# Wider token tiles and a swapped copy of the queries in the first stage of a vision tower

## The chip, the cores and the metric

The kernel runs on one core of one Trainium2 chip. The metric is device time in microseconds for one execution of the whole program; three runs of the kernel before gave 3623.95 to 3631.38 us, median 3631.38.

## The reference

Sixty-four images of 224 x 224 become 196 tokens each (patches of 16 x 16 x 3, 768 values, embedded to 256 channels), then comes one attention block with a relative-position term and one mixture-of-experts block. What the first stage has to compute is this, cut to what matters:

```python
h = einsum('bnp,dp->bnd', patches, W) + b                     # h0
x = layernorm(h)
Q, K, V = x @ Wq, x @ Wk, x @ Wv                              # 16 heads of 16 dims
term1 = einsum('bhqd,bhkd->bhqk', Q, K)
term2 = einsum('bhqd,kd->bhqk', Q, r)                         # r: sin and cos of the distance
term3 = einsum('hd,bhkd->bhk', u, K)
term4 = einsum('hd,kd->hk', v, r)
scores = (term1 + term3 + rel_shift(term2 + term4)) / sqrt(16)
```

Since r holds sines and cosines of a distance, the terms on r are computed as a rotation of the query: each dimension of Q + v is multiplied by one table, its partner dimension (8 further on, modulo 16) by another, and the two products are added. Everything is handed on as a bf16 high half and a bf16 low half, so that three bf16 products give nearly fp32.

## The kernel before

`tower` runs six stages one after the other; `project` (L112) is the first and the only one that the diff touches. It works through 32 positions of 392 tokens (two images, PAIR). Each engine has its own list of instructions, written by hand, with waits on semaphores; nothing reorders them. `positions` (L194) runs `position(n, u)` for n = 0 to 32, u = n modulo 2 choosing the buffer. In a position the engines do the following, in the order of their lists.

- TensorE: transposes the normalised rows xn(n) into psT (L457); embeds the tokens of n + 1 (four tiles of 98 tokens, 72 products of 256 columns, into psH); sums per head the products of Q + u with the next token's key for n - 1 (L469, into a corner of psT called psC); then values V(n) into psJ1 (24 products of 256 columns), keys K(n) into psJ0 (12 of 392), and per half m of the channels the queries and the queries with swapped dimensions (L472 onward, 24 of 392). The swapped queries come from a second set of weight columns.
- ScalarE: casts psT to nh, splits the next x into its high half xh, casts the rotated halves of n - 1 (L288), copies V to v32 (L294), casts K (L300), takes the standard deviation for n + 1 (L273), copies K in fp32 (k32), casts the queries (QH, L309).
- VectorE: nl = psT - nh; xl = x - xh (L334); then `normalise(n + 1)`: adds the token bias to psH, giving h0 (L339), statistics, their aggregation (L343, L349), waits for ScalarE's standard deviation, takes the reciprocal and writes xn with four `tensor_scalar` instructions (L356); copies psC to c32 (L371); then `rotate(n)`: per half m four terms from the two query tiles in PSUM (L385), the products with the shifted keys (L393) and the low half of the query (L397).
- GpSimd: low half of K (L416), and per half m the sum of the terms (L419) and, after ScalarE's cast, its low half (L421).
- The SP queue: stores of h0 and of v, the load of x for n + 4, the store of c, and last the store of the stack of rotated halves, each as soon as its wait allows, in this order (L227 to L240). So the store of h0 for n waits in the queue behind the stack of n - 1.

Two of VectorE's waits decide the order around the change: h0 of n + 1 may only be written when the store of n - 1 has landed, and rotate of n only starts when GpSimd has written the low halves of n - 1:

```python
dve.wait_ge(h0_out.sems[u], h0_out.at(n - 2, u))
dve.wait_ge(abl_ok.sem, abl_ok.at(n - 1))
```

At the start ScalarE waits for all seven weight and table loads before its first cast.

## Time and profile before

| what | value |
|---|---|
| median of three runs | 3631.38 us (3623.95 to 3631.38) |
| profiled execution | 3636.08 us, span 3634.4 us |
| mean granted TensorE clock | 0.939 |
| busy over the span: TensorE, VectorE, ScalarE, GpSimd | 89%, 72%, 41%, 45% |
| first stage | from 0 to about 675 us |

The page divides the span into 40 slices; the first seven, some 640 us, are the first stage, with TensorE at nine tenths or more from the second on. A share over the whole span says little about this stage, so windows and the timeline of the stage itself are read. A busy time on the timeline is from the start of an instruction to its end, and instructions of one engine that follow each other may overlap by some 0.1 us; where a sum matters, the spacing of starts is used.

### The profile page before, as it was taken

The page shows a single profiled execution, that of the slowest core. Times are in us where ns is not written, and L with a number is a line of the kernel's source. Part 1 is how long each engine was busy: PE and PEld are TensorE (multiplying, and loading weights), DVE is VectorE, ACT ScalarE, POOL GpSimd, SP SyncE. Part 2 cuts the span into 40 slices and gives each one's busy share as a digit, 9 for nine tenths or more (in the row PEclk, how much of TensorE's full clock was granted, in tenths as well). Part 3 has the DMA queues.
Part 4 walks back from the last instruction along what each step waited for, and adds up shares of the span by engine and source line. Part 5 has one row for each costly group of instructions (what it writes and reads, how often), then busy time and mean ns, then how long its engine had stood idle before and what let it go on. Part 6 is the DMA issues. An engine that isn't in the chain of part 4 may idle for free. (4 is left out here: it accounts for less than half of the span.)

```text
span 3634.4 us, 89293 instructions
## 1 busy us (share of the span) xinstructions
PE 3229.9 (89%) x34825; PEld 2526.0 (70%) x34881; DVE 2623.7 (72%) x6129; ACT 1498.6 (41%) x2991; POOL 1617.8 (45%) x1965
## 2 busy tenths in 40 slices
PE   6999999399999999999996722999599999998997
PEld 6888887378888888888883311778377777775876
DVE  5888888568888888888884676554266666665887
ACT  3444444056666666666663310332133333332221
POOL 2555555256666666666662010577200000004776
PEclk9999999579999999999998855999799999998999
DMA  4666665736556565665654611354333333225776
GB/s 141 185 185 197 195 186 161 189 84 164 157 149 172 136 166 148 160 162 148 170 133 131 182 30 34 110 140 126 95 116 111 107 104 106 95 90 135 217 219 165
DMA packets 449244, 518.11 MB, mean 143 GB/s; under 512 B 64150, under 2 KB 418804, under 8 KB 448397
## 3 DMA queue, kind: packets, MB, share of 16 engines
q1 hardware_dynamic: 427376, 473.19, 46.1%
q0 software_dynamic: 21504, 39.94, 4.1%
...
q14 instruction: 119, 0.97, 0.1%
HBM read 306.93 MB, written 215.94 MB: 144 GB/s over the span
## 5 line engine op out<-in xcount | busy, mean ns | idle before, releaser
L1281 POOL DMA_INDIRECT sb_ye<-scratch_ye,sb_table x224 | 240.8, 1075 | 805.6 <-DMA sb_gw<-scratch_gw 733.3
L854 DVE TENSOR_REDUCE p_mx<-p_psS 98x2 f32<-98x390 f32 (+1 forms) x1024 | 527.1, 556 | 0.0
L800 ACT ACTIVATE p_after<-p_psF 98x392 f32<-98x392 f32 x512 | 255.1, 498 | 480.6 <-PE p_psF L946 472.5
L803 ACT ACTIVATE p_probs<-p_psE 98x392 f32<-98x392 f32 x1024 | 450.1, 496 | 0.0
L848 DVE COPY_PREDICATED p_psS<-p_later,p_psD 98x196 f32<-98x196 uint32 x1024 | 330.6, 362 | 120.0 <-PE p_psS L932 111.4
L749 POOL TENSOR_SCALAR_AFFINE_SELECT p_after<-p_after 98x392 f32<-98x392 f32 x512 | 274.4, 536 | 243.2 <-ACT p_after L800 243.0
L1269 POOL DMA_INDIRECT scratch_xe<-sa_xs,sa_table x224 | 222.2, 992 | 205.6 <-DMA sa_xs<-scratch_xf 140.4
L753 POOL TENSOR_SCALAR_AFFINE_SELECT p_probs<-p_probs 98x392 f32<-98x392 f32 x512 | 274.5, 536 | 85.8 <-ACT p_probs L803 80.2
L969 PE MATMUL p_psO<-p_probs,p_v 98*32 98x196 f32 x4096 | 279.8, 345 | 2.0 <-POOL p_probs L753 1.7
L419 POOL TENSOR_TENSOR p_rt<-p_rt 128x784 f32<-128x784 f32 x64 | 187.1, 2924 | 122.7 <-DVE p_st L397 122.7
L103 PE MATMUL p_psH<-p_wh,p_xh 128*98 128x256 bf16 x768 | 211.5, 275 | 24.3 <-DVE p_xl L334 24.3
L916 PE MATMUL p_psD<-p_K,p_U 96*98 96x98 bf16 (+1 forms) x2048 | 187.8, 215 | 36.7 <-DVE p_later L835 29.0
L916 PEld LDWEIGHTS p_psD<-p_K,p_U 96*98 96x98 bf16 x2048 | 160.6, 128 | 73.4 <-DVE p_later L835 29.1
L103 PE MATMUL p_psH<-p_wl,p_xh 128*98 128x256 bf16 x768 | 211.3, 275 | 0.0
L103 PE MATMUL p_psH<-p_wh,p_xl 128*98 128x256 bf16 x768 | 211.2, 275 | 0.0
L946 PE MATMUL p_psF<-p_U,p_K 98*98 98x98 bf16 x2048 | 180.3, 211 | 28.8 <-DMA p_U<-p_mrow 28.8
L1387 DVE CAST ex_gh<-ex_g 128x512 bf16<-128x512 f32 (+1 forms) x256 | 106.3, 415 | 106.7 <-ACT ex_g L1322 87.4
...
L1389 DVE TENSOR_TENSOR ex_gl<-ex_g,ex_gh 128x512 bf16<-128x512 f32 (+1 forms) x256 | 171.4, 669 | 8.8
L1322 ACT ACTIVATE ex_g<-ex_psG,ex_b 128x512 f32<-128x512 f32 (+1 forms) x128 | 85.7, 669 | 219.7 <-PE ex_psG L103 219.7
L1322 ACT ACTIVATE ex_g<-ex_psG,ex_first_b 128x512 f32<-128x512 f32 (+1 forms) x128 | 85.7, 669 | 218.1 <-PE ex_psG L103 218.1
L946 PEld LDWEIGHTS p_psF<-p_U,p_K 98*98 98x98 bf16 x2048 | 147.5, 127 | 32.5 <-DMA p_U<-p_mrow 31.6
(300 smaller groups left out, 10110.7 us busy)
## 6 DMA issues: line engine op xcount, KB each, us to landing
...
```

The lines of the kernel that those rows point to most:

```text
L103: last = nc.tensor.matmul(out, a, b, start=start and k == 0, stop=stop and k == len(todo) - 1)
L749: nc.gpsimd.affine_select(after[c][:], after[c][:], pattern=[[0, 4], [-1, TILE]], compare_op=ALU.is_ge, fill=nothing, base=-2, channel_mul ...
L753: nc.gpsimd.affine_select(diagonal, diagonal, pattern=[[0, 4], [1, TILE]], compare_op=ALU.is_ge, fill=nothing, base=0, channel_multiplier= ...
L800: act.activation(after[c][:].rearrange("p h t -> p (h t)"), psF[:, 0:4 * TILE], ACT.Exp, scale=DK ** -0.5).then_inc(p_ok.sem, 1)
L803: act.activation(probs[c][:, b, :], psE[:, b, 0:PAIR], ACT.Exp, scale=DK ** -0.5).then_inc(p_ok.sem, 1)
L848: nc.vector.copy_predicated(own[:, :, c * TILE:(c + 1) * TILE], later[:].unsqueeze(1).broadcast_to([TILE, 2, TILE]), upper).then_inc(chose ...
L854: nc.vector.tensor_reduce(mx[g1][:, c, 4 * q1 + 2 * b:4 * q1 + 2 * b + 2], own, AX.X, ALU.max).then_inc(s_max.sem, 1)
L916: last = nc.tensor.matmul(psD[:, j * TILE:j * TILE + wide], U[u][0:STACK, h][:, mid], K[u][0:STACK, h][:, mid.start + 1:mid.start + 1 + wi ...
L946: last = nc.tensor.matmul(psF[:, j * TILE:(j + 1) * TILE], K[u][0:ROWS, h][:, mid], U[u][0:ROWS, h][:, mid], start=True, stop=True)
L969: nc.tensor.matmul(psO[32 * j:32 * j + 32, 0:S], v32[u][:, 2 * g + c, 4 * q + j, :], probs[c][:, j // 2, (j % 2) * S:(j % 2 + 1) * S], sta ...
L1269: nc.gpsimd.indirect_dma_start(out=d["xe"], out_offset=bass.IndirectOffsetOnAxis(ap=table[:, b * BLOCK + t, k:k + 1], axis=0), in_=xs[v][: ...
L1281: nc.gpsimd.indirect_dma_start(out=ye[v][u][:, t, k, :], out_offset=None, in_=d["ye"], in_offset=bass.IndirectOffsetOnAxis(ap=table[:, at ...
```

## The change

The embedding, the statistics and the values now work on tiles of 112 tokens: even positions bring in four tiles (448 tokens), odd ones three (336). nh and nl become one ring of two positions: `new[u]` is what a position brings in, `own[u]` the 392 tokens whose keys and queries it computes. TensorE no longer computes the swapped queries; the weight columns for them stay in memory unused. Since the dimensions lie eight heads apart, the partner dimension lies 64 partitions away, and ScalarE makes the swapped copy `qsw` in SBUF with two activations of 64 partitions per half m. The keys are cast from k32, after the queries.

The rows' normalisation goes from VectorE to ScalarE: VectorE makes the reciprocal and the shift nmr = -mean x rstd, ScalarE writes xn with scale and bias. VectorE's rotation of n - 1 now lies in position n, its first half ahead of nl(n), its second behind it, and the moments come before xl. GpSimd adds both halves' terms before it subtracts either. At the start the token weights and the first x are loaded ahead of the rest, and the first embedding waits for their casts alone.

VectorE, one position in the loop (p_h is h0, p_psJ the queries, p_rt the terms, p_st the stack). Before:

```order
L363 TENSOR_TENSOR p_nl<-p_psT,p_nh 128x784
L334 TENSOR_TENSOR p_xl<-p_x,p_xh 128x2352
L339 TENSOR_TENSOR p_h<-p_psH,p_tokb 98x1024
L343 BN_STATS p_stats<-p_h 98x6 x4
L349 BN_AGGR p_mv<-p_stats 98x2 x4
L352 RECIPROCAL p_rstd<-p_std 98x4
L356 TENSOR_SCALAR p_xn<-p_h,p_mv,p_rstd 98x256 x4
L371 COPY p_c<-p_psT 98x64
L385 SCALAR_TENSOR_TENSOR p_rt<-p_psJ,p_cols,p_rot 128x392 x4
L393 SCALAR_TENSOR_TENSOR p_prod<-p_psJ,p_cols,p_k 128x392
L397 SCALAR_TENSOR_TENSOR p_st<-p_psJ,p_cols,p_st 128x392
```

And now, from nl on:

```order
L386 TENSOR_TENSOR p_nl<-p_psT,p_nh 128x2x336
L401 REGISTER_ALU
L407 SCALAR_TENSOR_TENSOR p_prod<-p_psJ,p_cols,p_k 128x392
L404 SCALAR_TENSOR_TENSOR p_rt<-p_psJ,p_cols,p_rot 128x392 x2
L415 MEMSET p_prod 128x4
L416 SCALAR_TENSOR_TENSOR p_st<-p_psJ,p_cols,p_st 128x392
L404 SCALAR_TENSOR_TENSOR p_rt<-p_qsw,p_cols,p_rot 128x392 x2
L357 ISA
L359 TENSOR_TENSOR p_h<-p_psH,p_tokb 112x1024
L363 BN_STATS p_stats<-p_h 112x6 x4
L368 BN_AGGR p_mv<-p_stats 112x2 x4
L373 RECIPROCAL p_rstd<-p_std 112x4
```

The second half of the rotation stands between nl and the bias addition, the four xn instructions are gone, and two of the terms read p_qsw.

ScalarE, one position in the loop. Before:

```order
L281 ACTIVATE p_nh<-p_psT 128x784
L268 ACTIVATE p_xh<-p_x 128x2352
L288 ACTIVATE p_st<-p_rt 128x2x392
L294 ACTIVATE p_v<-p_psJ 98x1024
L288 ACTIVATE p_st<-p_rt 128x2x392
L300 ACTIVATE p_st<-p_psJ 128x2x392
L273 ACTIVATE p_std<-p_mv,p_eps 98x4
L306 ACTIVATE p_k<-p_psJ 128x2x392
L309 ACTIVATE p_st<-p_psJ,p_cols 128x392 x2
```

And now, from the standard deviation of one position to nh of the next:

```order
L282 ACTIVATE p_std<-p_mv,p_eps 112x3
L309 ACTIVATE p_v<-p_psJ 112x1024
L288 ACTIVATE p_xn<-p_h,p_nmr,p_rstd 112x256 x3
L317 ACTIVATE p_k<-p_psJ 128x2x392
L321 ACTIVATE p_st<-p_psJ,p_cols 128x392
L324 ACTIVATE p_qsw<-p_psJ 64x392
L325 ACTIVATE p_qsw<-p_psJ 64x392
L321 ACTIVATE p_st<-p_psJ,p_cols 128x392
L324 ACTIVATE p_qsw<-p_psJ 64x392
L325 ACTIVATE p_qsw<-p_psJ 64x392
L327 ACTIVATE p_st<-p_k 128x2x392
L297 ACTIVATE p_nh<-p_psT 128x2x336
```

The standard deviation has moved ahead of the values' copy, xn and the swapped copies are new, and the cast of the keys stands last.

The diff, cut to its core:

```diff
+WIDE = 112
...
+        def count(u):
+            return 4 - u
+
+        def tokens(u):
+            return WIDE * count(u)
...
+        nh, nl = sb("nh", [128, 2, 2 * PAIR], BF16), sb("nl", [128, 2, 2 * PAIR], BF16)
+        new = [slice(0, tokens(0)), slice(tokens(0), 2 * PAIR)]
+        own = [slice(u * PAIR, (u + 1) * PAIR) for u in range(2)]
+        qsw = sb("qsw", [128, 2, PAIR])
...
+                def load(n, u):
+                    sp.dma_start(x32[u][:], d["x"][:, :, bass.ds(n * PAIR + 56 * u, tokens(u))]).then_inc(x_in.sems[u], 16)
+
+                sp.dma_start(w32[:], d["tok_w"]).then_inc(w_in, 16)
+                load(0, 0)
...
+                    rows, new_rows = bass.ds(n * PAIR, PAIR), bass.ds(n * PAIR + 56 * u, tokens(u))
...
-                    sp.dma_start(tiles_of(d["h0"][rows, :]), h0[u][:]).then_inc(h0_out.sems[u], 16)
+                    sp.dma_start(tiles_of(d["h0"][new_rows, :], WIDE), h0[u][:]).then_inc(h0_out.sems[u], 16)
...
+                    act.wait_ge(t_ok.sem, t_ok.at(n - 1))
+                    for t in range(count(u)):
+                        last = act.activation(xn[:, t, :], h0[u][:, t, :], ACT.Identity, bias=nmr[:, t:t + 1], scale=rstd[:, t:t + 1])
+                    last.then_inc(xn_ok.sem, 1)
...
+                    if known(n, 1, PAIRS + 1):
+                        for m in range(2):
                             act.wait_ge(ab_ok.sem, ab_ok.at(n - 1, m + 1))
                             act.activation(st[1 - u][:, m, AH:BH + 1:2, :], rt[:, m, 0:4:2, :], ACT.Copy).then_inc(abh_ok.sem, 1)
-
-                    halves(0)
+                    if known(n, 0, PAIRS - 1):
+                        deviation(n + 1, 1 - u)
...
+                    if known(n, 0, PAIRS - 1):
+                        normalise(n + 1, 1 - u)
...
-                        act.wait_ge(st_out.sems[u], st_out.at(n - 2, u))
-                        act.activation(st[u][:, :, KH, :], psJ[0][:, :, 0:PAIR], ACT.Copy).then_inc(kh_ok.sem, 1)
-                    if known(n, 0, PAIRS - 1):
-                        deviation(n + 1)
-                    if known(n, 0, PAIRS):
...
                         act.activation(k32[:, :, 0:PAIR], psJ[0][:, :, 0:PAIR], ACT.Copy).then_inc(k32_ok.sem, 1)
...
                         for m in range(2):
...
-                            act.activation(st[u][:, m, QH, :], psJ[(m + 1) % 2][:, 0, 0:PAIR], ACT.Identity,
+                            act.activation(st[u][:, m, QH, :], psJ[1][:, m, 0:PAIR], ACT.Identity,
                                            bias=cols[:, m, 0:1]).then_inc(qh_ok.sem, 1)
-
+                            act.wait_ge(rt_ok.sem, rt_ok.at(n - 1, m + 1))
+                            act.activation(qsw[0:64, m, :], psJ[1][64:128, m, 0:PAIR], ACT.Copy)
+                            act.activation(qsw[64:128, m, :], psJ[1][0:64, m, 0:PAIR], ACT.Copy).then_inc(qsw_ok.sem, 1)
+                        act.wait_ge(k32_ok.sem, k32_ok.at(n))
+                        act.activation(st[u][:, :, KH, :], k32[:, :, 0:PAIR], ACT.Copy).then_inc(kh_ok.sem, 1)
...
+                act.wait_ge(w_in, 16)
+                act.activation(wh[:], w32[:], ACT.Copy).then_inc(w_hi, 1)
+                split(0, 0)
+                act.wait_ge(loaded, 16 * 6)
...
+                    nc.vector.tensor_tensor(h0[u][:], psH[:, 0:count(u)], tokb[:].unsqueeze(1).broadcast_to([WIDE, count(u), C]),
...
-                    for t in range(4):
-                        last = nc.vector.tensor_scalar(xn[:, t, :], h0[u][:, t, :], mv[:, t, 0:1], rstd[:, t:t + 1],
-                                                       ALU.subtract, ALU.mult)
-                    last.then_inc(xn_ok.sem, 1)
...
+                    nc.vector.reciprocal(rstd[:, 0:count(u)], std[:, 0:count(u)]).then_inc(recip_ok.sem, 1)
+                    dve.wait_ge(recip_ok.sem, recip_ok.at(n))
+                    nc.vector.scalar_tensor_tensor(nmr[:, 0:count(u)], mv[:, 0:count(u), 0], -1.0, rstd[:, 0:count(u)],
+                                                   ALU.mult, ALU.mult).then_inc(rstd_ok.sem, 1)
...
+                    if known(n, 1, PAIRS + 1):
+                        dve.wait_ge(k32_ok.sem, k32_ok.at(n - 1))
+                        dve.wait_ge(abl_ok.sem, abl_ok.at(n - 2))
+                        dve.wait_ge(st_out.sems[1 - u], st_out.at(n - 3, 1 - u))
+                        rotate(n - 1, 1 - u, 0)
...
+                        nc.vector.tensor_tensor(nl[:, :, new[u]], psT[:, :, 0:tokens(u)], nh[:, :, new[u]], ALU.subtract).then_inc(nl_ok.sem, 1)
+                    if known(n, 1, PAIRS + 1):
+                        rotate(n - 1, 1 - u, 1)
+                    if known(n, 0, PAIRS - 1):
+                        moments(n + 1, 1 - u)
                     if known(n, 0, PAIRS - 2):
                         split(n + 2, u)
-                    if known(n, 0, PAIRS - 1):
-                        normalise(n + 1, 1 - u)
...
-                    if known(n, 0, PAIRS):
-                        rotate(n, u)
...
-                    for m in range(2):
-                        qa, qb = psJ[(m + 1) % 2][:, 0, 0:PAIR], psJ[(m + 1) % 2][:, 1, 0:PAIR]
-                        dve.wait_ge(jq_ok.sem, jq_ok.at(n, m + 1))
-
...
-                        term(1, qb, 2)
-                        term(3, qb, 2)
-                        dve.wait_ge(qh_ok.sem, qh_ok.at(n, m + 1))
-                        term(0, qa, 1)
-                        term(2, qa, 1)
-                        last = nc.vector.scalar_tensor_tensor(prod[:, m, :], qa, cols[:, m, 0:1], k32[:, m, 1:PAIR + 1],
...
+                def rotate(n, u, m):
+
+                    q, swapped = psJ[1][:, m, 0:PAIR], qsw[:, m, :]
+                    dve.wait_ge(qsw_ok.sem, qsw_ok.at(n, m + 1))
...
+                    last = nc.vector.scalar_tensor_tensor(prod[:, m, :], q, cols[:, m, 0:1], k32[:, m, 1:PAIR + 1],
+                                                          ALU.add, ALU.mult)
+                    if m:
+                        last.then_inc(prods.sem, 1)
+                    term(0, q, 1)
+                    term(2, q, 1)
+                    if m:
+                        dve.wait_ge(prods.sem, prods.at(n))
+                        nc.vector.memset(prod[:, :, S - 1:PAIR:S], NEVER / DK).then_inc(prod_ok.sem, 1)
+                    nc.vector.scalar_tensor_tensor(st[u][:, m, QL, :], q, cols[:, m, 0:1], st[u][:, m, QH, :],
+                                                   ALU.add, ALU.subtract).then_inc(q_used.sem, 1)
+                    term(1, swapped, 2)
+                    term(3, swapped, 2).then_inc(rt_ok.sem, 1)
...
-                        pool.wait_ge(q_used.sem, q_used.at(n, m + 1))
+                        pool.wait_ge(rt_ok.sem, rt_ok.at(n, m + 1))
                         nc.gpsimd.tensor_tensor(rt[:, m, 0:4:2, :], rt[:, m, 0:4:2, :], rt[:, m, 1:4:2, :], ALU.add).then_inc(ab_ok.sem, 1)
+                    for m in range(2):
                         pool.wait_ge(abh_ok.sem, abh_ok.at(n, m + 1))
                         nc.gpsimd.tensor_tensor(st[u][:, m, AL:BL + 1:2, :], rt[:, m, 0:4:2, :],
                                                           st[u][:, m, AH:BH + 1:2, :], ALU.subtract).then_inc(abl_ok.sem, 1)
...
+                pe.wait_ge(w_lo, 1)
...
+                    for t in range(count(u)):
+                        cut = slice(t * WIDE, (t + 1) * WIDE)
...
-                        (gh[:, c, col:col + 128], gl[:, c, col:col + 128], nh[:, c, :], nl[:, c, :]) for c in range(2)])
+                        (gh[:, c, col:col + 128], gl[:, c, col:col + 128], nh[:, c, own[u]], nl[:, c, own[u]]) for c in range(2)])
...
-                        pe.wait_ge(q_used.sem, q_used.at(n - 1, 1))
-                        for t in range(4):
...
+                        pe.wait_ge(qsw_ok.sem, qsw_ok.at(n - 1))
+                        for t in range(count(u)):
...
-                        pe.wait_ge(q_used.sem, q_used.at(n - 1))
+                        pe.wait_ge(k32_ok.sem, k32_ok.at(n - 1))
...
-                            if m:
-                                pe.wait_ge(k32_ok.sem, k32_ok.at(n))
-                            ps = psJ[(m + 1) % 2]
-                            rows(ps[:, 0, 0:PAIR], 128 * m)
-                            rows(ps[:, 1, 0:PAIR], C + 128 * m).then_inc(jq_ok.sem, 1)
+                            rows(psJ[1][:, m, 0:PAIR], 128 * m, u).then_inc(jq_ok.sem, 1)
...
+                pe.wait_ge(w_lo, 6)
```

## Rows read from the trace of the kernel before

**Rows 1.** Windows: us, busy us (instructions) of PE, PEld, DVE, ACT, POOL, clock, DMA share, GB/s.
```profile
200.00:400.00 200.00, 196.31 (x1641) 166.91 (x1640) 169.18 (x313) 86.39 (x103) 117.17 (x53) 1.00 0.64 193
```

**Rows 2.** Timeline of VectorE: start us, us, engine, line, instruction, idle before it.
```profile
343.42 2.76 DVE L356 TENSOR_SCALAR p_xn<-p_h,p_mv,p_rstd 98x256 f32<-98x256 f32 x4
346.11 0.21 DVE L371 COPY p_c<-p_psT 98x64 f32<-98x64 f32 x1
346.24 2.21 DVE L385 SCALAR_TENSOR_TENSOR p_rt<-p_psJ,p_cols,p_rot 128x392 f32<-128x392 f32 x4
...
352.83 0.98 DVE L363 TENSOR_TENSOR p_nl<-p_psT,p_nh 128x784 bf16<-128x784 f32 x1
...
356.48 1.23 DVE L339 TENSOR_TENSOR p_h<-p_psH,p_tokb 98x1024 f32<-98x1024 f32 x1
357.74 1.41 DVE L343 BATCH_NORM_STATS2 p_stats<-p_h 98x6 f32<-98x256 f32 x4
359.33 0.38 DVE L349 BATCH_NORM_AGGREGATE p_mv<-p_stats 98x2 f32<-98x6 f32 x4 [0.18 <-DVE p_stats L343]
362.28 0.18 DVE L352 RECIPROCAL p_rstd<-p_std 98x4 f32<-98x4 f32 x1 [2.57 <-ACT p_std L273]
...
566.47 1.23 DVE L339 TENSOR_TENSOR p_h<-p_psH,p_tokb 98x1024 f32<-98x1024 f32 x1
```

**Rows 3.** Timeline of TensorE, values, keys and queries of one position.
```profile
299.74 0.27 PE L103 MATMUL p_psJ<-p_gh,p_nl 128*98 128x256 bf16 x1
...
301.81 0.33 PE L103 MATMUL p_psJ<-p_nh,p_gh 128*128 128x392 bf16 x1
...
305.62 0.33 PE L103 MATMUL p_psJ<-p_nh,p_gl 128*128 128x392 bf16 x1
```

**Rows 4.** Waits from 100 to 600 us: us in total, times, longest.
```profile
DVE p_rstd L352 <- ACT p_std L273: 65.3, 26, 2.6
...
PEld p_psT L457 <- DVE p_xn L356: 11.1, 14, 0.8
...
DVE p_h L339 <- DMA scratch_h<-p_h: 0.2, 1, 0.2
```

**Rows 5.** Timeline of GpSimd and, between its rows, VectorE's xl.
```profile
344.04 1.68 POOL L416 TENSOR_TENSOR p_st<-p_k,p_st 128x784 bf16<-128x784 f32 x1 [0.34 <-ACT p_k L306]
...
368.76 1.84 POOL L419 TENSOR_TENSOR p_rt<-p_rt 128x784 f32<-128x784 f32 x1 [3.89 <-DVE p_st L397]
371.57 1.67 POOL L421 TENSOR_TENSOR p_st<-p_rt,p_st 128x784 bf16<-128x784 f32 x1 [0.97 <-ACT p_st L288]
372.69 3.01 DVE L334 TENSOR_TENSOR p_xl<-p_x,p_xh 128x2352 bf16<-128x2352 f32 x1
373.20 4.22 POOL L419 TENSOR_TENSOR p_rt<-p_rt 128x784 f32<-128x784 f32 x1
```

**Rows 6.** Timeline of ScalarE.
```profile
340.18 1.02 ACT L294 ACTIVATE p_v<-p_psJ 98x1024 f32<-98x1024 f32 x1 [6.86 <-PE p_psJ L103]
...
342.89 0.29 ACT L273 ACTIVATE p_std<-p_mv,p_eps 98x4 f32<-98x4 f32 x1
...
344.16 0.59 ACT L309 ACTIVATE p_st<-p_psJ,p_cols 128x392 bf16<-128x392 f32 x1 [0.27 <-PE p_psJ L103]
...
351.48 0.86 ACT L288 ACTIVATE p_st<-p_rt 128x784 bf16<-128x784 f32 x1 [1.10 <-POOL p_rt L419]
```

**Rows 7.** Timeline of the SP queue, and the bias addition that waited for a store.
```profile
613.86 1.02 SPq L240 DMA_DIRECT2D scratch_stack<-p_st  x2
614.93 1.42 SPq L227 DMA_DIRECT2D scratch_h<-p_h  x1
...
622.47 1.23 DVE L339 TENSOR_TENSOR p_h<-p_psH,p_tokb 98x1024 f32<-98x1024 f32 x1 [1.86 <-DMA scratch_h<-p_h]
```

**Rows 8.** Timeline of the stage's start, ScalarE's first cast and TensorE's first product.
```profile
13.29 1.48 ACT L260 ACTIVATE p_wh<-p_w 128x1536 bf16<-128x1536 f32 x1 [10.66 <-DMA p_blk<-in_blk]
...
24.28 0.42 PE L103 MATMUL p_psH<-p_wh,p_xh 128*98 128x256 bf16 x1 [24.28 <-DVE p_xl L334]
```

144 lines of the change are left out of this document (63 added, 81 removed).

## The prediction

> **What bounds the kernel now.** The change touches the first stage alone, so I read that stage first by windows: from 200 to 400 us TensorE is busy 196.3 of 200 us at a granted clock of 1.00, VectorE 169.2, ScalarE 86.4, GpSimd 117.2, with the DMA engines at 0.64 [rows 1]. Then the period of one position, from VectorE's timeline: the addition of the token bias starts at 356.48 and, eleven positions later, at 566.47, so one position takes 19.09 us [rows 2]. Third, what TensorE does in it. Nineteen products with 256 moving columns start between 299.74 and 301.81, 0.109 us each, and 23 with 392 columns between 301.81 and 305.62, 0.166 us each [rows 3]. A position has 96 of the first (10.46 us) and 36 of the second (5.96 us); transposes, head sums and short waits are the other 2.7 us. Fourth, the waits: TensorE's wait for the normalised rows is 11.1 us over some 26 positions, and VectorE itself loses 65.3 us, 2.5 us a position, to ScalarE's standard deviation, which stands there behind other casts [rows 4]. TensorE is the bound, VectorE is some 2.5 us behind it.
>
> **What TensorE loses.** Over two positions seven tiles of 112 replace eight of 98. The tile is the stationary side, so a product costs its 256 columns whatever the tile's width: 18 products a tile in the embedding and 6 in the values give 24 x 0.5 x 0.109 = 1.31 us a position. The swapped queries are 12 products of 392 columns: 1.99 us. One transpose in sixteen goes and each is a seventh wider; I take that as nothing. TensorE's need falls by 3.30 us, to 15.79 us a position if its present waits stay. That is a floor, for VectorE's round may now be longer.
>
> **VectorE's new round.** VectorE runs its list in order, so its round is its work plus its waits. From [rows 2], with 7/8 where a position has 3.5 tiles instead of 4: the twelve three-operand instructions with their memset 6.59 us (346.24 to 352.83), nl 0.98, bias 1.08, statistics 1.23, their aggregation with its wait 0.51, reciprocal 0.21, c 0.13. The low half xl shows 3.01 us from 372.69 to 375.70, but GpSimd's subtraction held it until 373.24 [rows 5], so 2.46. Not shown before is the small shift instruction nmr; it handles 4 elements like the reciprocal, which takes 0.18, and I take 0.20 (between nothing, if it overlaps, and 0.35, a quarter of the 1.41 for statistics of 4 x 256 elements). The four normalising instructions, 2.76 us, go. Work: 13.4 us.
>
> Four of the twelve now read the swapped query from SBUF and not from PSUM. The rows show no such form; between 0.41 us (392 elements at xl's 1.05 ns) and 0.61 I leave them at 0.53, the spacing of the present ones.
>
> The waits, from a walk over one position with these durations, time 0 at the transposes:
> - ScalarE, which has two more activations of half the partitions per query half, makes the high half of q, then the swapped copy of the first half by about 0.4, of the second by 1.7, the high half of k by 2.5, nh by 3.3. Prices are from [rows 6]: 0.59 for 392 elements with a bias; a swapped half the same or a little less, 0.50; 1.02 for 1024; 0.86 for 784 from SBUF; 0.29 for 4 elements. An xn tile of 256 elements lies between 0.29 and 0.59; I take 0.50, and 0.41 from one start to the next.
> - The first rotation starts at 0.4, and its two swapped terms come up at about 2.6. GpSimd has taken its k subtraction at 2.5, for 1.67. I count 1.2 us for this block (0 to 1.67).
> - nl and the second rotation end at about 9.2; the bias addition follows. Its buffer must have been stored. The store is issued behind the stack's: 613.86 stack, 614.93 store, 622.47 landed and the addition let go after 1.86 us idle [rows 7], so 8.6 us from the stack's issue. Before, the addition starts 10.2 us after the copy of c, at which the position begins (356.48 from 346.32), and the store is waited for once, 0.2 us [rows 2, 4]. At 9.2 it will be late in some positions: 0.4 us on average (0 to 1.2).
> - Standard deviation: ScalarE reaches it ahead of the values' copy, so the wait falls from 2.5 us to the 0.29 us and two hand-overs, 0.4.
> - xl finds GpSimd in its subtractions or takes the pair itself: 0.25. In the latter case the last subtraction waits for xl, and the next first rotation waits for it (it needs the previous low halves written): 1.67 less what c covers, in about every second position, 0.95 (0 to 1.7).
>
> 13.4 + 1.2 + 0.4 + 0.4 + 0.25 + 0.95 = 16.6 us. ScalarE's list, 8.2 us a position before (86.4 over 10.5 positions), gets 1.5 us of xn and 1.7 of swapped copies and stays under 12 us. It matters only as a link. GpSimd's five instructions are the same.
>
> The blocks rest on the trace: GpSimd's addition of terms takes 1.84 us alone and 4.22 beside xl, where it ends 1.7 us after xl does; the normalising instructions take 2.76 with GpSimd's k subtraction inside them [rows 2, 5]. xl has both inputs in SBUF, and so have the four terms on the swapped query. If they were not shut out as xl is, the round would be 15.4 us, and TensorE's 15.8 would bind. The Trainium skill states this in SBUF — State Buffer, "Who interferes with whom": a VectorE instruction with two SBUF inputs and a GpSimd instruction that reads SBUF exclude each other for their whole length. The rows agree (4.22 = 2.4 of wait + 1.84). By that rule the swapped query in SBUF makes four new instructions that can be shut out, which speaks against this change.
>
> **Start and end.** Now ScalarE's first cast waits for the last of seven loads until 13.29 and the first embedding starts at 24.28 [rows 8]. After, two transfers stand ahead: 0.79 MB of weights and 1.38 MB of x, of the 2.8 MB that had landed by 13.3, so about 10 us; cast 2.5 and low half 2.8 of a tile set 8/7 as wide: start at about 15.3, 9 us earlier (5 to 10.5, if the loads share the engines). At the end the two swapped copies stand in the last rotation's way: 1.8 us later.
>
> **Sum.** Thirty full intervals x (19.09 - 16.6) = 75, plus 9, less 1.8: 82 us. The profiled execution took 3636.08 us (span 3634.4), 4.7 above the median of 3631.38, so 3554 of its kind and about 3550 us against the median.
>
> **Rivals.**
> - TensorE stays the bound, 15.8 us a position: the blocks fall beside other waits. For it: each wait above is a fraction of a GpSimd instruction, and their order may settle. Against it: odd and even positions differ (the embedding is 3 tiles long in one and 4 in the other), so in one of them the head sums wait for the second rotation. 30 x 3.30 + 7 = 106: 3525 us. Chance 0.22.
> - The stores bind: the bias addition waits for h0's store in every position, and the next stack's issue follows from it. Such a round is 8.6 us from stack to landing, 3.0 for the moments, 0.4 + 0.4, xl 2.5, c and the queue 0.7, and the blocked last subtraction 1.7: 17.3 to 18, say 17.7. 30 x 1.4 + 6 = 48: 3583 us. The DMA engines, 0.64 x 19.09 = 12.2 us of work a position, would be at 0.70 and do not bind by themselves. Chance 0.16.
> - Slower: VectorE and GpSimd exclude each other throughout. GpSimd has 2 x 1.84 + 3 x 1.67 = 8.7 us a position. If VectorE sat out all of it, 13.4 + 8.7 + 0.8 = 22.9 us, 30 x 3.8 - 7 = 107 us more: 3740 us. It decides from 4.9 us of block a position on (19.09 - 13.4 - 0.8). For it: one new-form pair directly behind each k subtraction. Against it: two of GpSimd's five wait for VectorE's own terms, and 1.4 to 3 us is what I find. Chance 0.05.
> - The change doesn't shorten the round: some ordering wait between the swapped copies and TensorE's next values holds it at 19 us. The values wait for the second rotation's low half, at about 8.4, with TensorE there at 9.4; 1 us is spare. Start alone: 3624 us. Chance 0.03.
>
> The forecast has the other 0.54. Its own range, by the bounds of the blocks (16.1 to 17.2), is 3532 to 3569. For eight in ten I take 3520 to 3590, which holds most of the first two rivals. A measurement of this kernel tells 0.2% (7 us) from no change; faster by more than that 0.92, within it 0.03, slower 0.05.
>
> A rule on the price of sources: VectorE: DVE Perf Modes, the section on the TRN2 errata, gives a VectorE instruction that reads PSUM 62 cycles more of fixed cost than one from SBUF; for four instructions that would be an estimated 0.26 us a position off the round, 8 us off the time. No row of before shows it, and the sum goes without it.
>
> **What would show it.** In the profile of the changed kernel: period near 16.6 us between bias additions; TensorE at some 92% of the steady windows with waits on c, on the products and on the copy of v; the idle time before the reciprocal about 0.4; the first two swapped terms of a position beside GpSimd's k subtraction and longer than the others; a DMA wait in front of the bias addition in some positions; first embedding at 15 us; the later stages as they were. Wrong would be: swapped terms without any lengthening (then 3525), a DMA wait in each position (3583), or a granted clock under 1.00 in the steady stretch, since TensorE now waits more often than before.

## The result, and the profile after

The changed kernel took 3612.77 us (median of 7 runs, 3600.89 to 3624.29), the kernel before 3626.25 beside it: a ratio of 0.995, 95% interval 0.9938 to 0.9963. The forecast was 3550, its range ended at 3590: the change helps, but by 13 us between the medians (18 by the ratio) instead of some 80. The profiled execution took 3608.68 us (span 3606.9), 27.4 less than the profiled one of before, which was 10 us above its median; the one of after was 4 below.

Where these 27.4 us lie is read from the bias additions, one a position. Three rows of before, not shown so far, are the first and the third addition and VectorE's first instruction of the next stage:

```profile
34.41 1.23 DVE L339 TENSOR_TENSOR p_h<-p_psH,p_tokb 98x1024 f32<-98x1024 f32 x1 [7.87 <-PE p_psH L103]
...
70.09 1.21 DVE L339 TENSOR_TENSOR p_h<-p_psH,p_tokb 98x1024 f32<-98x1024 f32 x1
...
675.76 2.67 DVE L829 MEMSET p_K<- 3x3136 uint32 x1 [14.89 <-issue]
```

The same of after, with the third addition and the last of the 32, and TensorE's first product:

```profile
16.25 0.43 PE L104 MATMUL p_psH<-p_wh,p_xh 128*112 128x256 bf16 x1 [16.25 <-DVE p_xl L353]
```

```profile
26.40 1.22 DVE L359 TENSOR_TENSOR p_h<-p_psH,p_tokb 112x1024 f32<-112x1024 f32 x1
...
57.59 1.21 DVE L359 TENSOR_TENSOR p_h<-p_psH,p_tokb 112x1024 f32<-112x1024 f32 x1
...
590.55 0.95 DVE L359 TENSOR_TENSOR p_h<-p_psH,p_tokb 112x768 f32<-112x768 f32 x1
...
646.60 2.67 DVE L853 MEMSET p_K<- 3x3136 uint32 x1 [16.16 <-issue]
```

The start gives 8.0 us (34.41 to 26.40; 24.28 of [rows 8] is now 16.25). The 31 intervals took 588.06 us before (to the last addition, 622.47, [rows 7]) and take 564.15: 23.9 us. The end of the stage costs 2.8 (53.29 to 56.05), the later stages 1.6. That 1.6 says nothing: the later stages, which no edit touches, last from 2952 to 2975 us in the profiles of this document, so the interval is a finer measure of the first stage than the whole time. From the third addition on, the 29 intervals are 18.38 us on average, against 19.05 before (19.09 over the eleven of [rows 2]) and the 16.6 of the forecast. So nearly all that is missing is in the steady round.

The window that answers to [rows 1], and one that holds just those 29 intervals:

```profile
200.00:400.00 200.00, 179.65 (x1396) 157.54 (x1395) 161.06 (x281) 124.94 (x185) 107.65 (x54) 0.92 0.63 191
57.59:590.55 532.96, 475.13 (x3784) 415.00 (x3783) 436.04 (x757) 344.71 (x507) 288.36 (x145) 0.95 0.64 193
```

No engine is the bound now. From 200 to 400 us TensorE is at 90% and its granted clock at 0.92, where it was 1.00. Over the 29 intervals VectorE is busy 436.04 us, 15.0 each. The forecast had 13.4 of work, 1.2 of a block and 0.25 at xl, 14.85: VectorE's work came out about as reckoned, its waits did not. They were to be 1.75 us and are 3.3. (From 200 to 400 us the intervals are longer, 18.83 on average from 203.68 to 391.97, so that window holds fewer than 200 / 18.38 of them.) VectorE's timeline over two positions, answering to [rows 2]:

```profile
345.30 0.63 DVE L407 SCALAR_TENSOR_TENSOR p_prod<-p_psJ,p_cols,p_k 128x392 f32<-128x392 f32 x1 [4.33 <-ACT p_qsw L325]
...
353.93 1.21 DVE L359 TENSOR_TENSOR p_h<-p_psH,p_tokb 112x1024 f32<-112x1024 f32 x1
...
357.80 1.41 DVE L375 SCALAR_TENSOR_TENSOR p_nmr<-p_mv,p_rstd 112x4 f32<-112x4 f32 x1
...
363.56 0.62 DVE L407 SCALAR_TENSOR_TENSOR p_prod<-p_psJ,p_cols,p_k 128x392 f32<-128x392 f32 x1 [2.04 <-ACT p_qsw L325]
...
365.70 2.57 DVE L404 SCALAR_TENSOR_TENSOR p_rt<-p_qsw,p_cols,p_rot 128x392 f32<-128x392 f32 x2
...
371.35 1.15 DVE L404 SCALAR_TENSOR_TENSOR p_rt<-p_qsw,p_cols,p_rot 128x392 f32<-128x392 f32 x2
372.42 0.94 DVE L359 TENSOR_TENSOR p_h<-p_psH,p_tokb 112x768 f32<-112x768 f32 x1
...
375.87 0.20 DVE L375 SCALAR_TENSOR_TENSOR p_nmr<-p_mv,p_rstd 112x3 f32<-112x3 f32 x1
```

GpSimd beside it:

```profile
336.28 6.09 POOL L447 TENSOR_TENSOR p_st<-p_rt,p_st 128x784 bf16<-128x784 f32 x2
...
355.89 3.30 POOL L447 TENSOR_TENSOR p_st<-p_rt,p_st 128x784 bf16<-128x784 f32 x2
...
366.12 1.74 POOL L441 TENSOR_TENSOR p_st<-p_k,p_st 128x784 bf16<-128x784 f32 x1 [6.92 <-ACT p_st L327]
```

The first half's two swapped terms last 2.57 us beside the k subtraction, the second half's 1.15: a block of 1.42, forecast 1.2. The shift (nmr) takes 0.20 us in one position and 1.41 in the other, where it meets GpSimd's two subtractions; forecast 0.20 throughout. The Trainium skill states (SBUF — State Buffer, "Who interferes with whom") that a VectorE instruction with two SBUF inputs and a GpSimd instruction that reads SBUF exclude each other; the trace agrees down to four elements a partition, where the sum had not applied it. And the first rotation waits 4.33 and 2.04 us for the swapped copies. It was to start 0.4 us behind the transposes; these start at 344.26 and 361.57, so it starts 1.0 and 2.0 us behind them:

```profile
344.26 0.74 PE L483 MATMUL p_psT<-p_ident,p_xn 112*128 112x112 f32 x6
...
361.57 0.98 PE L483 MATMUL p_psT<-p_ident,p_xn 112*128 112x112 f32 x8 [1.22 <-DVE p_c L396]
```

ScalarE ahead of the first of the two waits, answering to [rows 6]:

```profile
340.57 1.02 ACT L309 ACTIVATE p_v<-p_psJ 112x1024 f32<-112x1024 f32 x1 [3.17 <-PE p_psJ L104]
341.49 1.57 ACT L288 ACTIVATE p_xn<-p_h,p_nmr,p_rstd 112x256 f32<-112x256 f32 x3
342.97 0.80 ACT L317 ACTIVATE p_k<-p_psJ 128x784 f32<-128x784 f32 x1
343.68 0.57 ACT L321 ACTIVATE p_st<-p_psJ,p_cols 128x392 bf16<-128x392 f32 x1
344.27 0.49 ACT L324 ACTIVATE p_qsw<-p_psJ 64x392 f32<-64x392 f32 x1
344.78 0.49 ACT L325 ACTIVATE p_qsw<-p_psJ 64x392 f32<-64x392 f32 x1
```

ScalarE waits for the values, then works without a gap through the copy of v, the rows, k32, the first queries and their swapped copy, 4.7 us, and 345.30 is the moment at which VectorE goes on. Ahead of the second wait its rows start late, at 359.25, since they wait 1.11 us for the long shift. The waits from 100 to 600 us, answering to [rows 4]:

```profile
DVE p_prod L407 <- ACT p_qsw L325: 64.1, 25, 4.3
...
PE p_psT L495 <- DVE p_prod L415: 36.2, 14, 2.6
...
DVE p_rstd L373 <- ACT p_std L282: 16.1, 27, 0.7
...
DVE p_prod L407 <- POOL p_st L447: 3.4, 2, 1.7
...
DVE p_h L359 <- DMA scratch_h<-p_h: 1.0, 2, 0.6
```

And TensorE, whose head sums wait 2.6 us behind the embedding of three tiles, with windows of that stretch (columns of [rows 1]):

```profile
371.04 2.80 PE L495 MATMUL p_psT<-p_blk,p_prod 128*98 128x8 f32 x16 [2.58 <-DVE p_prod L415]
```

```profile
366.00:368.40 2.40, 2.40 (x23) 2.21 (x21) 2.40 (x3) 2.40 (x3) 1.78 (x2) 1.00 1.04 318
368.40:371.00 2.60, 0.06 (x1) 0.00 (x0) 2.60 (x6) 1.55 (x2) 1.80 (x1) 0.99 1.00 235
371.00:374.00 3.00, 2.96 (x18) 2.99 (x19) 2.96 (x6) 0.09 (x1) 1.42 (x1) 0.50 1.01 330
374.00:377.50 3.50, 3.50 (x18) 3.50 (x17) 2.61 (x8) 1.05 (x2) 3.50 (x3) 0.50 0.09 33
```

TensorE works at 2.4 GHz until 368.4, idles 2.6 us, and then runs for at least 6.5 us at 1.2 GHz. This comes in many pairs of positions, not in all, and in some the low clock is shorter; an interval with the long one is some 19.5 us, others are 17.3 to 18.5.

### The profile page after: what moved, and what is told of

The parts are those of the page before. It is cut to its first block and busy times, and to the rows that moved or that the text cites. A ratio compares the mean times of both kernels' runs of the same rounds, so it can differ in the third digit from the quotient of the medians.

```text
span 3606.9 us, 87936 instructions
## 1 busy us (share of the span) xinstructions
PE 3154.7 (87%) x34081; PEld 2473.8 (69%) x34081; DVE 2583.2 (72%) x6003; ACT 1611.8 (45%) x3233; POOL 1584.8 (44%) x1965
## 5 line engine op out<-in xcount | busy, mean ns | idle before, releaser
L104 PE MATMUL p_psH<-p_wh,p_xh 128*112 128x256 bf16 x672 | 184.6, 275 | 16.3 <-DVE p_xl L353 16.3
L104 PE MATMUL p_psH<-p_wl,p_xh 128*112 128x256 bf16 x672 | 184.4, 274 | 0.0
L104 PE MATMUL p_psH<-p_wh,p_xl 128*112 128x256 bf16 x672 | 184.2, 274 | 0.0
L997 PEld LDWEIGHTS p_psO<-p_after,p_v 98*32 98x32 f32 x4096 | 134.3, 111 | 38.5
```

Source lines behind the costliest of these rows:

```text
L104: last = nc.tensor.matmul(out, a, b, start=start and k == 0, stop=stop and k == len(todo) - 1)
L997: last = nc.tensor.matmul(psO[32 * j:32 * j + 32, c * TILE:(c + 1) * TILE], v32[u][:, 2 * g + c, 4 * q + j, :], after[c][:, j, :], start=F ...
```

## The experiments

Theory 1: a ring of waits over all engines closes the round (head sums, values, copy of v, rows, k32, queries, swapped copies, first rotation, nl, second rotation, head sums), GpSimd's blocks lie on it, and the low clock comes on top. Rivals: the low clock alone, TensorE's list, the stores. All runs were timed beside the kernel before, and ratios are to it; interval is the mean between bias additions, the 29 from the third to the last, and clock that of 200 to 400 us.

| run | edits on the changed kernel | us | ratio to before, 95% | interval | clock |
|---|---|---|---|---|---|
| – | the changed kernel | 3612.8 | 0.9950 (0.9938–0.9963) | 18.38 | 0.92 |
| 1 | products in TensorE's gap | 3591.0 | 0.9885 (0.9869–0.9902) | 18.03 | 0.98 |
| 2 | keys first | 3593.4 | 0.9901 (0.9887–0.9916) | 17.81 | 1.00 |
| 3 | k subtraction late | 3571.9 | 0.9845 (0.9832–0.9857) | 17.21 | 0.95 |
| 4 | shift by tile | 3599.5 | 0.9927 (0.9914–0.9940) | 18.01 | 0.97 |
| 5 | tiles of 98 | 3604.1 | 0.9931 (0.9914–0.9948) | 18.39 | 1.00 |
| 6 | 3 + 4 | 3575.2 | 0.9856 (0.9836–0.9877) | 17.36 | 0.97 |
| 7 | 2 + 3 + 4 | 3594.7 | 0.9902 (0.9882–0.9922) | 17.88 | 0.98 |
| 8 | rows by VectorE | 3568.1 | 0.9837 (0.9818–0.9857) | 17.17 | 1.00 |
| 9 | 3 + 8 | 3565.4 | 0.9824 (0.9810–0.9838) | 17.19 | 1.00 |
| 10 | 3 + 8, h0 stored early | 3563.3 | 0.9826 (0.9813–0.9839) | 17.01 | 0.97 |
| 11 | 10 with tiles of 98 | 3562.5 | 0.9822 (0.9808–0.9835) | 17.14 | 1.00 |
| 12 | 8, h0 stored early | 3580.5 | 0.9867 (0.9851–0.9882) | 17.61 | 0.97 |
| 13 | 10, c ahead of xl | 3552.9 | 0.9785 (0.9770–0.9800) | 16.68 | 0.98 |
| 14 | 13 with tiles of 98 | 3556.7 | 0.9799 (0.9786–0.9812) | 16.78 | 1.00 |
| 15 | c ahead of xl alone | 3623.3 | 0.9981 (0.9969–0.9993) | 18.65 | 0.92 |
| 16 | 3 + 8, c ahead of xl | 3551.5 | 0.9783 (0.9766–0.9799) | 16.65 | 0.98 |

**Run 1, products in the gap.**

```diff
+                    if known(n, 1, PAIRS) and u == 0:
+                        for k in range(24):
+                            nc.tensor.matmul(psT[:, 1, 448:512], wh[:, 0, 0:128], wh[:, 0, 0:64], start=True, stop=True)
                     if known(n, 1, PAIRS + 1):
                         pe.wait_ge(prod_ok.sem, prod_ok.at(n - 1))
```

> Adds work: in each even position, between the three-tile embedding and the wait for the head sums, TensorE makes 24 products of 64 columns into an unused corner of PSUM. In the changed kernel TensorE idles 2.6 us there and the granted clock is then 0.50 for some 6 us in most even positions, where the head sums take 2.74 us instead of 1.49. Theory 1 (the idle time brings the clock down, and the low clock costs 0.9 to 1.2 us a position on top of a round of some 17.6): the clock stays at or near 1.00 in the steady windows, the slow intervals of 18.5 and 19.6 us between bias additions go to 17.3 to 18.0, and the time falls by 20 to 36 us, to about 3580. It does not reach the 3550 forecast, since the undisturbed intervals are 17.3 to 18 already. Rival (the clock falls for another reason, or the low clock is hidden beside other waits): no change or slightly longer, 3605 to 3625.

TensorE's timeline, the added products and the head sums behind them:

```profile
326.51 0.87 PE L492 MATMUL p_psT<-p_wh 128*128 128x64 bf16 x24 [0.87 <-DVE p_nl L386]
328.12 1.55 PE L498 MATMUL p_psT<-p_blk,p_prod 128*98 128x8 f32 x16 [0.74 <-DVE p_prod L415]
```

The gap is cut into 0.87, 0.87 of work and 0.74, the head sums take 1.55 instead of 2.80, and a single interval, 19.53, is as long as those with the low clock were. The ratio falls by 0.0065 though work was added: that the low clock costs time is shown. In the steady round run 1 gets back 0.35 us a position, 10 us of the 22 between the medians; the rest lies outside these intervals. The round is 18.03, not 16.6, so the clock is the smaller part of the loss.

**Run 2, keys first.**

```diff
+                    if known(n, 0, PAIRS):
+                        pe.wait_ge(k32_ok.sem, k32_ok.at(n - 1))
+                        for m in range(2):
+                            last = rows(psJ[0][:, m, 0:PAIR], 2 * C + 128 * m, u)
+                        last.then_inc(jk_ok.sem, 1)
                     if known(n, 1, PAIRS + 1):
                         pe.wait_ge(prod_ok.sem, prod_ok.at(n - 1))
...
-                        pe.wait_ge(k32_ok.sem, k32_ok.at(n - 1))
-                        for m in range(2):
-                            last = rows(psJ[0][:, m, 0:PAIR], 2 * C + 128 * m, u)
-                        last.then_inc(jk_ok.sem, 1)
```

> TensorE makes the keys of a position ahead of the head sums and the values instead of behind the values, so 12 products of 392 columns (2.0 us) fill the idle time that stands there. Theory 1 (a ring of waits: head sums, values, ScalarE's copy of v, xn, k32, queries, swapped copies, rotation): the clock holds near 1.00 as with the added products, but the queries now come directly behind the values and ScalarE's copies of v and xn stand between them and their casts, so the clean round grows by some 0.5 us: 18.0 to 18.2 us against a mean of 18.4 now, 3600 to 3610. Rival (TensorE's list, and its clock, is the only limit): the 2 us of idle time and the low clock both go, 16.5 us a position, about 3555.

Wholly at 2.4 GHz, and with TensorE busy 88% from 200 to 400 us, the round is still 17.81, so the rival falls. The queries now wait 1.1 us a position for the copy of v (30.7 us in 29 waits). Both numbers lie a little under those of theory 1.

**Run 3, k subtraction late.**

```diff
-                    pool.wait_ge(kh_ok.sem, kh_ok.at(n))
-                    pool.wait_ge(k32_ok.sem, k32_ok.at(n))
-                    nc.gpsimd.tensor_tensor(st[u][:, :, KL, :], k32[:, :, 0:PAIR], st[u][:, :, KH, :], ALU.subtract).then_inc(kl_ok.sem, 1)
                     for m in range(2):
                         pool.wait_ge(rt_ok.sem, rt_ok.at(n, m + 1))
                         ...
+                        if m == 0:
+                            pool.wait_ge(kh_ok.sem, kh_ok.at(n))
+                            pool.wait_ge(k32_ok.sem, k32_ok.at(n))
+                            nc.gpsimd.tensor_tensor(st[u][:, :, KL, :], k32[:, :, 0:PAIR], st[u][:, :, KH, :], ALU.subtract).then_inc(kl_ok.sem, 1)
```

> GpSimd's k subtraction (1.74 us) stands behind its first addition of terms instead of ahead of it, so the first two terms on the swapped query, which take 2.57 us beside it and 1.15 elsewhere, find GpSimd idle. Theory 1 (this block of 1.4 us lies on the ring): the two terms take 1.15, GpSimd's subtraction falls beside nl and the second half's instructions that read PSUM, and the round is 0.5 to 0.8 us shorter, 15 to 24 us off, about 3590, the clock still falling. Rival (the block stands beside a wait of the same length, ScalarE's cast of the first half): the terms get shorter and the wait behind them longer, within 7 us of 3610.

VectorE's first-half terms, from PSUM and from SBUF:

```profile
307.52 1.15 DVE L404 SCALAR_TENSOR_TENSOR p_rt<-p_psJ,p_cols,p_rot 128x392 f32<-128x392 f32 x2
308.59 0.62 DVE L416 SCALAR_TENSOR_TENSOR p_st<-p_psJ,p_cols,p_st 128x392 bf16<-128x392 f32 x1
309.12 1.16 DVE L404 SCALAR_TENSOR_TENSOR p_rt<-p_qsw,p_cols,p_rot 128x392 f32<-128x392 f32 x2
```

The block is gone and 1.17 us a position with it, more than theory 1 gave: one order on GpSimd is worth two to three times the whole change (0.0105 of the ratio against 0.0050, 41 us between medians against 13). The block lies on the ring for the most part; a part of the 1.17, less than the 0.35 of run 1, may be the clock's. The wait for the swapped copies stays all the same, 74.5 us in 29 waits: it is where the ring closes, and its length is not what a mended link gives back.

**Run 4, shift by tile.**

```diff
-                    nc.vector.scalar_tensor_tensor(nmr[:, 0:count(u)], mv[:, 0:count(u), 0], -1.0, rstd[:, 0:count(u)],
-                                                   ALU.mult, ALU.mult).then_inc(rstd_ok.sem, 1)
+                    for t in range(count(u)):
+                        last = nc.vector.tensor_scalar(nmr[:, t:t + 1], mv[:, t, 0:1], rstd[:, t:t + 1], -1.0, ALU.mult, ALU.mult)
+                    last.then_inc(rstd_ok.sem, 1)
```

> The shift nmr is made by one instruction per tile with one SBUF tensor and a scalar operand each (three or four of them) instead of one instruction with two SBUF tensors. In the changed kernel that small instruction takes 0.20 us where GpSimd is idle and 1.41 where it starts in GpSimd's two subtractions, and ScalarE's xn waits up to 1.1 us for it. Theory 1 (it is shut out by GpSimd like the large ones, and it lies on the ring by way of xn, k32 and the queries): the long form goes, each of the small ones takes some 0.1 to 0.2 us, and the round is 0.3 to 0.5 us shorter, 8 to 16 us off, 3595 to 3600. Rival (xn waits for the copy of v anyway): no change, within 7 us of 3610.

```profile
315.33 0.58 DVE L376 TENSOR_SCALAR p_nmr<-p_mv,p_rstd 112x1 f32<-112x1 f32 x4
```

Four small instructions inside GpSimd's two subtractions take 0.58 us, not 1.41, and the round falls by 0.37: as theory 1 had it. Part of that may be the clock (0.97).

**Run 5, tiles of 98.**

```diff
-WIDE = 112
+WIDE = TILE
...
-            return 4 - u
+            return 4
...
```

> Undoes one part: four tiles of 98 tokens in every position, as before; the rest of the change stays. TensorE gets 24 x 0.5 x 0.109 = 1.31 us a position more in products, and its even positions no longer have the short embedding ahead of which it idles. Theory 1 (the round is a ring over all engines, whose sizes in VectorE and ScalarE are the same on average with 98 as with 112; TensorE has some 2 us a position to spare in the changed kernel, part of it lost to the low clock): the granted clock holds at 1.00, the round is 18.0 to 18.6 us, and the time is within 10 us of the changed kernel's 3613. Rival (TensorE's products set the time): 1.31 x 30 = 39 us more, 3650.

The clock holds at 1.00 and nearly every interval is 18.36 to 18.38: no slower than with 112. (The offsets of the loads and stores, not shown, are set to match.) The 1.31 us of products that the wide tiles save a position are given back as idle time and low clock.

**Runs 6 and 7, sums of edits** (the diffs of 3 and 4; of 2, 3 and 4).

> Both edits that each made the changed kernel faster: GpSimd's k subtraction behind its first addition of terms (17.21 us a position by itself), and the shift in one instruction per tile. Theory 1 (both blocks lie on the ring): their gains add, 0.4 us a position below the first edit alone, 16.7 to 16.9 us, 3557 to 3562. Rival (with the first block gone TensorE, with its need of 15.8 us and the low clock, binds): the shift is worth nothing here, 3567 to 3575.

> The two edits of the kernel before, and the keys ahead of the head sums. Theory 1 (what is left is the low clock): with the keys in the idle time the clock holds at 1.00 and the round comes to the forecast of 16.6 us, 3550. Rival (the queries directly behind the values wait for ScalarE's copy of v, 1.1 us of wait in each position as in the kernel with the keys moved alone, which had 17.81): the clock holds, but the round stays at 17.0 to 17.3, 3565 to 3575.

In 6 the shift adds nothing to run 3; the rival's time holds, at its upper end. In 7 both theories miss: the queries' wait for v is there as in 2 (30.5 us in 29 waits), and the gain of 3 is lost. VectorE's longest waits there are 43.1 us for the swapped copies, 17.5 for the embedding and 13.4 for h0's store; why they come together was not followed further.

**Run 8, rows by VectorE.**

```diff
...
-                    if known(n, 0, PAIRS - 1):
-                        normalise(n + 1, 1 - u)
...
-                    nc.vector.scalar_tensor_tensor(nmr[:, 0:count(u)], mv[:, 0:count(u), 0], -1.0, rstd[:, 0:count(u)],
-                                                   ALU.mult, ALU.mult).then_inc(rstd_ok.sem, 1)
+                    dve.wait_ge(t_ok.sem, t_ok.at(n - 1))
+                    for t in range(count(u)):
+                        last = nc.vector.tensor_scalar(xn[:, t, :], h0[u][:, t, :], mv[:, t, 0:1], rstd[:, t:t + 1],
+                                                       ALU.subtract, ALU.mult)
+                    last.then_inc(xn_ok.sem, 1)
```

> Undoes one part: VectorE writes the normalised rows itself again (three or four instructions of some 0.6 us, no shift instruction), ScalarE's three or four of 0.50 us between the copy of v and k32 go. Theory 1 (ScalarE's chain of v, xn, k32, queries, swapped copies lies on the ring): the chain gets 1.5 to 2.0 us shorter, VectorE's round 2.2 us longer less the shift (0.2 to 1.4): a round of 17.5 to 18.5, within 15 us of 3613. Rival (ScalarE is only a link without weight, VectorE's work sets the round): 0.6 x 3.5 - 0.8 = 1.3 us a position more, 3650.

VectorE's timeline, the rows of two positions, a first rotation and a bias addition:

```profile
302.51 1.38 DVE L365 TENSOR_SCALAR p_xn<-p_h,p_mv,p_rstd 112x256 f32<-112x256 f32 x4
...
305.97 0.22 DVE L387 COPY p_c<-p_psT 98x64 f32<-98x64 f32 x1
306.10 0.62 DVE L398 SCALAR_TENSOR_TENSOR p_prod<-p_psJ,p_cols,p_k 128x392 f32<-128x392 f32 x1
...
318.75 1.06 DVE L365 TENSOR_SCALAR p_xn<-p_h,p_mv,p_rstd 112x256 f32<-112x256 f32 x3
...
332.83 1.23 DVE L348 TENSOR_TENSOR p_h<-p_psH,p_tokb 112x1024 f32<-112x1024 f32 x1 [1.43 <-DMA scratch_h<-p_h]
```

This part of the change, undone, makes the kernel 45 us faster (41 by the ratios; the shift of run 4 goes with it); both theories gave less. The first rotation follows the copy of c without a wait, as the forecast had it, the clock is 1.00, and the rows cost VectorE 1.06 to 1.38 us, where [rows 2] had 2.76 with GpSimd's subtraction inside them. (In run 16, where GpSimd's subtractions come beside them again, they cost 1.38 to 2.42.) What waits now is the bias addition, 45.5 us in 27 positions for h0's store: the stores rival of the prediction, at 17.17 us instead of 17.7.

**Runs 9 to 12, the store.** h0 of n + 1 stored ahead of the stack of n (10 to 12; that of position 0 ahead of the loop):

```diff
-                    sp.wait_ge(h0_ok.sem, h0_ok.at(n))
-                    sp.dma_start(tiles_of(d["h0"][new_rows, :], WIDE), h0[u][:]).then_inc(h0_out.sems[u], 16)
+                    if known(n, 0, PAIRS - 1):
+                        store_h0(n + 1, 1 - u)
```

> The rows written by VectorE as in the run before, and GpSimd's k subtraction behind its first addition of terms. With the rows on VectorE the round was 17.17 us, the clock 1.00, and the bias addition waited 1.7 us in each position for h0's store, which stands in the SP queue behind the stack. Theory 2 (with ScalarE's chain off the ring the stores close it): taking the block of GpSimd away lengthens that wait instead, 17.0 to 17.2 us, within 7 us of 3568. Rival (the block still lies on the ring, since the stack waits for GpSimd's last subtraction): 0.5 us a position less, 3553.

> The rows written by VectorE, and the store of h0 for n + 1 issued ahead of the stack of n instead of behind it. Theory 2 (the stores close the ring): the bias addition's wait of 1.7 us a position goes and the round falls to what TensorE needs, 15.8 to 16.2 us: 30 to 40 us less than 3568, about 3533. Rival (that wait only stands in place of the waits on ScalarE's moments, GpSimd's block or TensorE): the wait goes and others grow, 16.8 to 17.1, 3558 to 3568.

> All three edits: rows by VectorE, the k subtraction behind the first addition, the store of h0 ahead of the stack. Theory 2: TensorE binds at some 15.8 us a position with the clock at 1.00, 3525 to 3535, the time that the prediction gave for TensorE as the bound. Rival (VectorE's and GpSimd's blocks at the swapped terms stay): 16.3 to 16.6, 3540 to 3550.

> The kernel with all three edits, but with four tiles of 98 in each position. In the changed kernel itself the width of the tiles made no difference that a run could tell. Theory 2 (now TensorE binds, so its products count): 1.31 us a position more than with 112, a round of 17.1 us, some 39 us more, about 3570. Rival (something else still sets the round): the same time as with 112 within 10 us.

Run 9 is as theory 2 had it. Run 12 is not: the store's wait goes, but the time rises. Run 10 goes to 15.6 and 17.76 us in turn, 19.42 with the low clock, and 11, with 98, is as fast. So the store's wait only stood in place of others, and with 112 TensorE doesn't bind (with 98, in run 11, it is busy 97% from 200 to 400 us): in run 10 it idles ahead of the transposes, which wait for the copy of c behind a long xl. Its transposes, the window behind them, and VectorE's xl:

```profile
321.11 1.35 PE L481 MATMUL p_psT<-p_ident,p_xn 112*128 112x112 f32 x6 [2.13 <-DVE p_c L393]
```

```profile
321.00:324.00 3.00, 2.90 (x15) 2.93 (x16) 3.00 (x6) 2.61 (x4) 0.00 (x0) 0.51 0.49 138
```

```profile
317.88 2.94 DVE L349 TENSOR_TENSOR p_xl<-p_x,p_xh 128x2688 bf16<-128x2688 f32 x1
```

**Runs 13 to 16, c ahead of xl.**

```diff
                     if known(n, 0, PAIRS - 1):
                         moments(n + 1, 1 - u)
-                    if known(n, 0, PAIRS - 2):
-                        split(n + 2, u)
                     if known(n, 1, PAIRS + 1):
                         ...
                         nc.vector.tensor_copy(c32[1 - u][:], psC).then_inc(c32_ok.sem, 1)
+                    if known(n, 0, PAIRS - 2):
+                        split(n + 2, u)
```

> The kernel with the three edits, and VectorE copies c ahead of xl instead of behind it. Without this TensorE waits for that copy ahead of the transposes in each position, 0.5 us in one and 2.1 in the other, and the clock is 0.50 for 2.2 us behind it in many of them. Theory 3 (that wait is the last one that keeps TensorE from binding): the transposes start 2 us earlier, the clock holds at 1.00, the round is 15.8 to 16.1 us, 3530 to 3540. Rival (VectorE's and GpSimd's work and blocks set the remaining round of 16.7): no gain, 3553 to 3563.

> The same with four tiles of 98. TensorE was busy for 97% of its 17.14 us there. Theory 3: only the remaining 3% can go, 16.7 to 16.9 us, 3550 to 3556, so with 112 the kernel is now 0.8 us a position faster than with 98. Rival (the width still makes no difference): within 7 us of the 112 tiles.

> The changed kernel with the copy of c ahead of xl as its only edit. TensorE waits some 1.2 us a position for that copy ahead of the transposes. Theory 1 (the ring of the changed kernel goes by ScalarE's rows, k32, the queries and the first rotation, and the transposes are only on it by way of nl): the wait goes over into a longer wait for the products ahead of the head sums, within 10 us of 3613, the clock lower if anything. Rival (TensorE's list is on the ring throughout): 1.2 us a position less, 3578.

> Rows by VectorE, the k subtraction late and c ahead of xl, but the store of h0 behind the stack as in the changed kernel. Theory 2 (with the rows on VectorE the store of h0 closes the ring at 17.2 us): no gain on the 3565 of the kernel without the c edit, within 7 us. Rival (the store waits are a cover of other waits): 16.0 to 16.5, 3535 to 3545.

Alone (15) the edit makes the changed kernel slower, by 10 us, with the clock at 0.92. The transposes now wait for ScalarE's rows instead of c (15.9 us in 14 waits), and the head sums wait as before (37.0 us, 36.2 in the changed kernel): the copy of c was not what held the ring. With the rows on VectorE it gains 14 us on run 9 (16), more than theory 2 allowed and less than its rival, and the early store adds nothing to it (13). Three successive bias additions of run 16, and TensorE ahead of an embedding:

```profile
304.65 0.94 DVE L348 TENSOR_TENSOR p_h<-p_psH,p_tokb 112x768 f32<-112x768 f32 x1
...
321.78 1.23 DVE L348 TENSOR_TENSOR p_h<-p_psH,p_tokb 112x1024 f32<-112x1024 f32 x1 [0.55 <-PE p_psH L104]
...
337.51 0.94 DVE L348 TENSOR_TENSOR p_h<-p_psH,p_tokb 112x768 f32<-112x768 f32 x1
```

```profile
313.61 0.29 PE L104 MATMUL p_psH<-p_wh,p_xh 128*112 128x256 bf16 x1 [1.91 <-issue]
```

Undisturbed pairs take 17.13 + 15.73, 16.43 us a position, and 18.79 stands for 17.12 where the clock falls. TensorE now idles ahead of the embedding; the profile names no releaser, but xl, which moved behind c, ends 0.1 us before that product (310.56 to 313.50). With 98 (14) it is busy 99% at full clock:

```profile
200.00:400.00 200.00, 198.55 (x1723) 177.98 (x1721) 185.92 (x357) 126.99 (x168) 103.22 (x60) 1.00 0.73 218
```

Its round of 16.78 is what theory 3 gave, but 112 is not 0.8 us better: the intervals of 13 and 14 overlap. The width of the tiles made no measurable difference in any of its three pairs (the changed kernel and 5, 10 and 11, 13 and 14). Run 16 is the simpler of the two fastest versions, 2.2% faster than before, 1.7% faster than the changed kernel.

One part of the change has no run of its own: none gives the swapped queries back to TensorE. So what the swapped copies cost by themselves, the 1.0 us of ScalarE ahead of the first rotation included, and whether they gain anything, isn't known.

## Why the prediction was wrong

- **TensorE's need, the start, the end:** right. The start gave 8.0 for 9, the end cost 2.8 for 1.8; TensorE's products are as counted, and TensorE is no longer the bound.
- **VectorE's busy time and the block by the k subtraction:** right in sum, 15.0 us for 14.85, partly by luck: the block is 1.42 for 1.2 and the shift some 0.6 over its term, xl and the rest of the rotation are a little under theirs.
- **The step that failed: "The first rotation starts at 0.4", and with it that ScalarE "matters only as a link".** The walk began at the transposes with VectorE just done with c and ScalarE free for the queries. This start state was assumed, not reached: ScalarE gets there only by way of the values, the copy of v and the rows, which the change itself had put between them and k32. The rotation starts 1.0 and 2.0 us behind the transposes, and VectorE, done with c, waits for the swapped copies 2.4 us a position (64.1 us in some 27 positions), a wait that the sum doesn't have. Run 8, where this wait is gone from the steady round, shows the price of moving the rows: 45 us.
- **The shift was mis-sized.** It has 0.20 us in the sum (0 to 0.35) and takes 0.80 on average over the 29 intervals, in most of them 0.20 or 1.41. "The four normalising instructions, 2.76 us, go" enters no term of the sum, which is made of what stays; but that row held GpSimd's k subtraction, and without one beside them the rows are 1.06 to 1.38 us (run 8). So half of the 2.76 was a block that the change moved to the swapped terms, where the sum counts it again, rightly.
- **Two waits that were forecast don't appear:** the stores (1.0 us in all for 0.4 a position) and GpSimd's last subtraction (3.4 in all for 0.95 a position), since the wait for ScalarE comes later than both: GpSimd's last subtraction ends at 342.37 (336.28 + 6.09), 2.9 us ahead of the rotation. So VectorE's 3.3 us of waits are 2.4 for the swapped copies (none in the sum), 0.6 for the deviation (0.4), 0.1 for the last subtraction (0.95) and 0.2 of small ones; 15.04 + 3.34 is the 18.38 of the profile.
- **The clock** was named as what would make the forecast wrong and had no price in it. It lengthens the same wait, since the values come later (4.05 to 4.33 us in the pairs with the long stretch at 1.2 GHz, 2.48 to 2.69 in the same place where it was shorter); run 1, nearly without it, has 18.03 us, so it is the smaller part, some 0.35 of 1.8.
- **The range** was narrower than the bounds beside its terms. Their upper ends, 1.67 for the block, 1.2 for the store and 1.7 for the last subtraction, add up to a round of 18.6 us, not 17.2. The measured 18.38 lies under that, but by a wait that none of them stands for.
- **Rivals:** nearest to what came is the fourth, an ordering wait that holds the round at 19 us (chance 0.03): 18.38 us. Its wait was looked for behind the swapped copies, at the next values; the one that came stands ahead of them. Slower by exclusion throughout did not come, the stores came only in runs 8 and 9. That TensorE stays the bound came in run 14 alone, with the narrow tiles. The forecast's round and time are reached, but by another kernel, run 16 (16.65 us, 3551 us), where the change's move of the rows is undone and two orders are mended.
